# Attention scores in 128 by 128 tiles with wrapped keys, one masking addition over two PSUM banks and one maximum over all four blocks

## The chip, the cores and the metric

The kernel runs on one core of a Trainium2 chip. The core has five engines that the program drives separately: PE (TensorE, matrix products into PSUM), DVE (VectorE), ACT (ScalarE), POOL (GpSimd) and SP (SyncE, which only issues DMAs here). Each engine takes its instructions strictly in program order, and they meet through semaphores alone. The metric is the device time of one execution, in microseconds (us); lower is better. Three executions of the kernel before took 4307.14, 4308.0 and 4308.48 us, median 4308.0.

## The reference, cut to what matters

The input is 16 sequences of 256 tokens with 128 channels. After a layer norm it goes two ways: through one state-space block, and through six layers of windowed attention and feed-forward; the results are multiplied and added to the input. The change concerns the attention of the six layers, with 16 heads of 64 channels and windows of 32 tokens:

```python
bq = q.reshape(b, h, nw, w, d)                   # w = 32, nw = 8
bk2 = look(bk); bv2 = look(bv)                   # the window before, and the window itself: 64 keys
mask = (it < jb) | (it > jb + w) | (jb == -1)    # a query sees itself and the 32 tokens before it
sim = jnp.einsum('bhwie,bhwje->bhwij', bq, bk2) * QK_SCALE
sim = jnp.where(mask, -jnp.finfo(sim.dtype).max, sim)
attn = jax.nn.softmax(sim, -1)
out = jnp.einsum('bhwij,bhwje->bhwie', attn, bv2)
```

So each query sees 33 keys: a band along the diagonal. Everything is in float32.

## The kernel before, in words

The first 500 us or so are the layer norm and the state-space block. Then come six layers over eight groups of two sequences (512 tokens), 48 items in all. They are worked on in a software pipeline, function `turn`: one turn of 16 steps has up to four items in flight, `next` (projections of q and k, their squares and the rotation), `cur` (scores and probabilities), `prev` (output projection, layer norm, first half of the feed-forward) and `prev2` (end of the feed-forward). Every engine has its own `turn` with its own order within the 16 steps; nothing reorders them. In step s one pair of heads p = s // 2 of one sequence b = s % 2 has its scores computed.

One such unit, the two heads (index i) of one sequence (two halves t of 128 queries), goes through these places:

- `scores(s)`, PE: eight products of 64 queries by 96 keys (`SCORE_TILES`), head 0 into bank 0, head 1 into bank 1. They wait for `sc_bias`, which says that the maxima of step s - 1 have been read, since there is one pair of score banks. The first 128 columns are keys 0 to 127 of queries 0 to 127, the next 160 (to `UW` = 288) are keys 96 to 255 of queries 128 to 255.
- `maxima(s)`, DVE: four fused instructions (line 1240, in the profile CUSTOM_DVE_ANT_0) that add the mask, write the sum to `sm` and reduce it to its maximum, each followed by an instruction that reads the accumulator out to `mx` in bank 1; then a small product that makes the bias `nb` of the exponential.
- `probabilities(s)`, ACT: four exponentials from `sm` to `pr`, each with its sum into `den` (line 852).
- `denominators(s - 2)`, DVE: one reciprocal, `rden` (line 1219).
- `normalise(s - 2)`, POOL: four products with `rden` (line 964).
- `transpose_probs(s - 3)`, PE: four transposes of 128 by 128 into bank 2 (lines 634, 635). They wait for `p_Tsb`, which says that bank 2 has been copied out.
- `copy_probs(s - 4)`, DVE: a 32 by 32 transpose per head straight from `pr` (line 1225), for the keys 96 to 127 that queries 128 to 159 see, and one copy of bank 2 to `pt` (line 1226).
- `outputs`, PE, every second step: probabilities times `vtok`.

Around these, in each step s, DVE runs in this order: `denominators(s - 2)`, `copy_probs(s - 4)`, `products(s - 1)` (two products of 128x512 from PSUM with the rotation tables, line 1194, which wait for the projection of q or k), then in some steps `residual`, `scale_q` and others, then `maxima(s)`, then in some steps `clamp`, `gated`, `split_high_x` and `split_low_x`. PE runs `scores(s)`, `project_out` in steps 2 to 5, `transpose_probs(s - 3)`, `outputs` or the value projection `make_v`, the projection of q or k with three passes (lines 290 to 292), and feed-forward products in steps 12 to 15. A projection waits until ACT has squared what lay in its bank (`square`, line 840). In step 7 PE centres the layer norm's input (line 670), which a DMA brings after DVE's `residual` of step 6.

## Time and profile before

| | |
|---|---|
| median of 3 executions | 4308.0 us |
| the profiled execution, its own time | 4310.28 us |
| its span, first to last instruction | 4308.2 us |
| granted TensorE clock, mean | 0.956 of full speed |
| busy: PE, DVE, ACT, POOL | 85%, 84%, 71%, 63% |
| reciprocals `rden`, one for each step with scores | 768, so 48 turns of 16 steps |

The profile counts an engine as busy while an instruction of it runs. DVE's instructions overlap a little: one can start before the last has ended, so the time that one takes of the engine is the distance to the next start, and not its duration. A product in float32 is shown as two PE instructions (a row of x16 is eight products). "Idle before, releaser" is time in which the engine stood still, and the instruction on another engine that ended the wait; "issue" is a wait for which the profile shows no releaser.

### The profile page before, as it was taken

How to read it: one execution, taken by the hardware profiler on the slowest of the kernel's cores; microseconds unless marked ns; L12 is line 12 of the kernel's file. 1: busy time of each engine (PE TensorE's matmuls, PEld its weight loads, DVE VectorE, ACT ScalarE, POOL GpSimd, SP SyncE). 2: the span in 40 equal slices, each digit the busy share in tenths (PEclk: the TensorE clock that was granted, in tenths of full speed). 3: DMA queues.
4: the chain of work that ended last, by engine and by line, in shares of the span. 5: the costliest groups of instructions: out<-in, count | busy, mean ns of one | idle time of the engine just before them, and what ended most of it. 6: DMA issues, size and time to landing. Idle time of an engine off the chain costs nothing. (4 is left out here: it accounts for less than half of the span.)

```text
span 4308.2 us, 109724 instructions
## 1 busy us (share of the span) xinstructions
PE 3648.7 (85%) x31072; PEld 2319.1 (54%) x31072; DVE 3618.5 (84%) x12131; ACT 3063.5 (71%) x8807; POOL 2732.3 (63%) x4419
## 2 busy tenths in 40 slices
PE   5887688898888888888988888888888888898884
PEld 2444355555555555555555555555555555555552
DVE  7999688889888888888888888888887888888873
ACT  3443477777777777777787777777776777877774
POOL 0000577777777777677776776777776767777771
PEclk8999799999999999999999999999999999999997
DMA  1000322222222222222222222222222222222221
GB/s 45 6 7 12 106 92 90 85 90 96 90 88 90 82 95 93 87 93 84 84 101 91 93 87 80 88 95 88 99 84 79 94 95 89 94 85 89 86 78 61
DMA packets 225228, 352.55 MB, mean 82 GB/s; under 512 B 41535, under 2 KB 68349, under 8 KB 224381
## 3 DMA queue, kind: packets, MB, share of 16 engines
q1 hardware_dynamic: 224604, 345.22, 23.4%
q8 instruction: 271, 4.44, 0.4%
q14 instruction: 353, 2.88, 0.2%
HBM read 125.41 MB, written 5.77 MB: 30 GB/s over the span
## 5 line engine op out<-in xcount | busy, mean ns | idle before, releaser
L964 POOL TENSOR_SCALAR pr<-pr,rden 128x128 f32<-128x128 f32 (+1 forms) x3072 | 1134.4, 388 | 931.7 <-DVE rden L1219 930.6
L852 ACT ACTIVATE pr<-sm,nb,rq 128x128 f32<-128x128 f32 (+1 forms) x3072 | 1515.9, 498 | 44.7 <-DVE nb L1246 39.4
L971 POOL TENSOR_TENSOR rot<-ab,swp 128x512 f32<-128x512 f32 x768 | 984.4, 1282 | 509.7 <-DMA swp<-ab 508.5
L1194 DVE TENSOR_TENSOR ab<-bank,ltab 128x512 f32<-128x512 f32 x1536 | 985.4, 683 | 281.3 <-PE bank L292 260.8
L1240 DVE CUSTOM_DVE_ANT_0 sm<-bank,mask 128x128 f32<-128x128 f32 (+1 forms) x3072 | 841.3, 330 | 55.9 <-issue 52.2
L840 ACT ACTIVATE sq<-bank 128x512 f32<-128x512 f32 x768 | 451.6, 588 | 256.7 <-DVE ab L1194 255.0
L852 ACT ACTIVATION_READ_ACCUMULATOR pr<-sm,nb,rq 128x1 f32 x3072 | 587.8, 191 | 0.0
L634 PE MATMUL bank<-ident,pr 128*128 128x128 f32 x1536 | 407.1, 291 | 210.1 <-DVE pt L1226 208.3
L1226 DVE COPY pt<-bank 128x512 f32<-128x512 f32 x768 | 531.5, 692 | 10.2
L625 PEld LDWEIGHTS bank<-rot 64*64 64x64 f32 x12288 | 291.9, 133 | 452.8 <-issue 452.4
L977 POOL TENSOR_TENSOR rot<-rot,rkb 128x512 f32<-128x512 f32 x384 | 497.7, 1296 | 44.2 <-DMA rkb<-k_scratch 44.2
L861 ACT ACTIVATE wide<-bank 128x512 f32<-128x512 f32 x384 | 228.6, 595 | 383.4 <-PE bank L653 383.1
L625 PE MATMUL bank<-rot 64*64 64x96 f32 x12288 | 435.8, 257 | 76.7 <-DVE nb L1246 41.7
L653 PE MATMUL bank<-pt,vtok 128*64 128x160 f32 (+1 forms) x6144 | 491.2, 305 | 0.0
L290 PE MATMUL bank<-xh,wqk_h 128*128 128x512 f32 x768 | 358.9, 467 | 118.1 <-ACT sq L840 97.6
L1240 DVE DVE_READ_ACCUMULATOR2_ANT bank<- 128x1 f32 x3072 | 437.3, 142 | 0.0
L653 PEld LDWEIGHTS bank<-pt,vtok 128*64 128x64 f32 x6144 | 389.7, 143 | 72.3 <-issue 68.9
L634 PEld LDWEIGHTS bank<-ident,pr 128*128 128x128 f32 x1536 | 220.3, 143 | 361.8 <-issue 321.7
L866 ACT ACTIVATE vtok<-bank 128x512 f32<-128x512 f32 x384 | 228.3, 595 | 230.4 <-PE bank L292 230.3
L635 PE MATMUL bank<-ident,pr 128*128 128x128 f32 x1536 | 390.1, 280 | 0.0
L664 PE MATMUL bank<-wide,wo 128*128 128x512 f32 x768 | 371.0, 605 | 0.9 <-ACT wide L861 0.9
L292 PE MATMUL bank<-xl,wqk_h 128*128 128x512 f32 x768 | 309.2, 403 | 0.0
(156 smaller groups left out, 6503.7 us busy)
## 6 DMA issues: line engine op xcount, KB each, us to landing
swp<-ab SPq DMA_DIRECT2D x1536, 128.0 KB, 2.0
rkb<-k_scratch SPq DMA_DIRECT2D x768, 128.0 KB, 2.9
raw<-Wqkv SPq DMA_DIRECT2D x48, 128.0 KB, 2.2
gg<-xT SPq DMA_DIRECT2D x48, 128.0 KB, 2.3
gg<-xT SPq DMA_DIRECT2D x48, 127.5 KB, 2.4
raw<-Wqkv SPq DMA_DIRECT2D x12, 256.0 KB, 2.7
wo<-Wo SPq DMA_DIRECT2D x6, 512.0 KB, 4.2
k_scratch<-rsum SPq DMA_DIRECT2D x192, 8.0 KB
```

The costliest lines, as they stand in the source:

```text
L625: mm = pe.matmul(bank[i][part, c:c + 96], rot[rows, p, c0 + 64 * half:c0 + 64 * half + 64], rot[rows, PAIRS + p, c0 + k0:c0 + k0 + 96], st ...
L634: pe.transpose(bank[2][:, 256 * i:256 * i + P], pr[:, e % 4, i, 0:P], ident[:, :])
L635: mm = pe.transpose(bank[2][:, 256 * i + P:256 * i + 2 * P], pr[:, e % 4, i, P + WINDOW:UW], ident[:, :])
L653: mm = pe.matmul(bank[3][64 * i:64 * i + 64, cols], vtok[:, 2 * b + t, ch], pt[:, e % 4, i, t, 0:cols.stop - cols.start], start=(b == 0 an ...
L840: act.activation(sq[:, j % NSQ, :], use_bank("qk", j)[:, :], ACT.Square).then_inc(qk_sq, 1)
L852: ins = act.activation(pr[:, s % 4, i, cs], sm[:, s % 2, i, cs], ACT.Exp, bias=nb[:, s, t, i:i + 1], scale=head_scale(rq, p, b)[:, t, i:i ...
L964: ins = pool.tensor_scalar(pr[:, e % 4, i, cs], pr[:, e % 4, i, cs], rden[:, e, t, i:i + 1], 1.0, ALU.mult, ALU.mult)
L971: pool.tensor_tensor(rot[:, PAIRS * (j % 2) + j // 2, :], ab[:, j % 2, 0, :], swp[:, j % 2, :], ALU.add).then_inc(qk_rot, 1)
L977: pool.tensor_tensor(rot[:, PAIRS + p, :], rot[:, PAIRS + p, :], rkb[:, p % KSLOT, :], ALU.mult)\
L1194: ins = dve.tensor_tensor(seqs(ab[:, j % 2, i, :]), seqs(use_bank("qk", j)[:, :]), ltab[:, 2 * (j % 2) + i:2 * (j % 2) + i + 1, :] .to_bro ...
L1226: dve.tensor_copy(pt[:, e % 4, :, :, 0:P], bank[2][:, :].rearrange("p (i t c) -> p i t c", i=2, t=2)).then_inc(p_Tsb, 1)
L1240: ins = dve.tensor_tensor_reduce(sm[:, s % 2, i, cs], bank[i][:, cs], mask[:, cs], 1.0, -3e38, ALU.add, ALU.max, mx[:, t, i:i + 1])
```

## The change

`SCORE_TILES` gets a fourth field, the number of keys of a tile. Queries 128 to 191 now have two tiles: 64 keys from 128 on, and the 32 keys 96 to 127, which are put behind, into the last 32 columns of their block ("wrapped"; those queries cannot see keys 224 to 255, whose place it is). Each of the four blocks of scores is then 128 by 128, and the scores of a head lie in 256 columns. Banks 0 and 1 become one tensor `pair`, so that one instruction can cover both.

`maxima` is one addition of the mask over both banks to `sm`, then one `tensor_reduce` over the last axis for all four maxima into `mx` in PSUM, then the product that makes `nb`. The reduction waits for the addition on a new semaphore `sc_mask`.

`copy_probs` ends with a `memset` of 32 partitions by 2x32 elements: after the transposes of PE the wrapped probabilities also stand in `pt` where keys 224 to 255 of queries 128 to 159 belong, and they must be zero there. The `memset` waits for the copy on a new semaphore `p_copy`, and it is now what releases `p_Tsb`. `normalise` is one product over all 512 elements with `rden` broadcast. The exponentials are all 128 wide.

```diff
-SCORE_TILES = [(0, 0, 0), (1, 32, 32), (2, P, P - WINDOW), (3, P + 64, P + 32)]
+SCORE_TILES = [(0, 0, 0, 96), (1, 32, 32, 96), (2, P, P, 64), (2, 2 * P - WINDOW, P - WINDOW, WINDOW), (3, P + WINDOW, P + WINDOW, 96)]
...
-        mask = sb("mask", [P, UW])
+        mask = sb("mask", [P, 2 * P])
...
-        bank = [ctx.enter_context(nc.psum_tensor(f"bank{i}", [P, GT], F32)) for i in range(8)]
+        pair = ctx.enter_context(nc.psum_tensor("pair", [P, 2, GT], F32))
+        bank = [pair[:, 0, :], pair[:, 1, :]]
+        bank += [ctx.enter_context(nc.psum_tensor(f"bank{i}", [P, GT], F32)) for i in range(2, 8)]
...
-        mx = bank[1][:, UW:UW + 4].rearrange("p (t i) -> p t i", t=2)
+        mx = pair[:, 1, 2 * P:2 * P + 4].rearrange("p (i t) -> p i t", i=2)
...
-                    for half, c, k0 in SCORE_TILES:
+                    for half, c, k0, kn in SCORE_TILES:
                         part = slice(64 * (half % 2), 64 * (half % 2) + 64)
                         for i in range(2):
                             rows = slice(64 * i, 64 * i + 64)
-                            mm = pe.matmul(bank[i][part, c:c + 96], rot[rows, p, c0 + 64 * half:c0 + 64 * half + 64],
-                                           rot[rows, PAIRS + p, c0 + k0:c0 + k0 + 96], start=True, stop=True)
+                            mm = pe.matmul(bank[i][part, c:c + kn], rot[rows, p, c0 + 64 * half:c0 + 64 * half + 64],
+                                           rot[rows, PAIRS + p, c0 + k0:c0 + k0 + kn], start=True, stop=True)
...
                         pe.transpose(bank[2][:, 256 * i:256 * i + P], pr[:, e % 4, i, 0:P], ident[:, :])
                         mm = pe.transpose(bank[2][:, 256 * i + P:256 * i + 2 * P],
-                                          pr[:, e % 4, i, P + WINDOW:UW], ident[:, :])
+                                          pr[:, e % 4, i, P:2 * P], ident[:, :])
...
-                            cs = slice(0, P) if t == 0 else slice(P, UW)
+                            cs = slice(t * P, t * P + P)
                             ins = act.activation(pr[:, s % 4, i, cs], sm[:, s % 2, i, cs], ACT.Exp,
...
-                    for i in range(2):
-                        for t in range(2):
-                            cs = slice(0, P) if t == 0 else slice(P, UW)
-                            ins = pool.tensor_scalar(pr[:, e % 4, i, cs], pr[:, e % 4, i, cs],
-                                                     rden[:, e, t, i:i + 1], 1.0, ALU.mult, ALU.mult)
+                    dst = pr[:, e % 4, :, 0:2 * P].rearrange("p i (t c) -> p i t c", t=2)
+                    ins = pool.tensor_tensor(dst, dst, rden[:, e, :, :].rearrange("p t i -> p i t").unsqueeze(3)
+                                             .to_broadcast([P, 2, 2, P]), ALU.mult)
...
-                    dve.transpose(pt[96:128, e % 4, :, 0, P:P + WINDOW], pr[0:32, e % 4, :, P:P + WINDOW])
+                    dve.transpose(pt[96:128, e % 4, :, 0, P:P + WINDOW], pr[0:32, e % 4, :, 2 * P - WINDOW:2 * P])
                     dve.tensor_copy(pt[:, e % 4, :, :, 0:P],
-                                    bank[2][:, :].rearrange("p (i t c) -> p i t c", i=2, t=2)).then_inc(p_Tsb, 1)
+                                    bank[2][:, :].rearrange("p (i t c) -> p i t c", i=2, t=2)).then_inc(p_copy, 1)
+                    dve.wait_ge(p_copy, n16 + (16 * q + e + 1))
+                    dve.memset(pt[96:128, e % 4, :, 1, 0:WINDOW], 0.0).then_inc(p_Tsb, 1)
...
-                    for i in range(2):
-                        for t in range(2):
-                            cs = slice(0, P) if t == 0 else slice(P, UW)
-                            ins = dve.tensor_tensor_reduce(sm[:, s % 2, i, cs], bank[i][:, cs], mask[:, cs],
-                                                           1.0, -3e38, ALU.add, ALU.max, mx[:, t, i:i + 1])
-                    ins.then_inc(sc_max, 1)
+                    dst = sm[:, s % 2, :, 0:2 * P]
+                    dve.tensor_tensor(dst, pair[:, :, 0:2 * P], mask[:, :].unsqueeze(1).to_broadcast([P, 2, 2 * P]),
+                                      ALU.add).then_inc(sc_mask, 1)
+                    dve.wait_ge(sc_mask, n16 + (s + 1))
+                    dve.tensor_reduce(mx, dst.rearrange("p i (t c) -> p i t c", t=2), AX_X, ALU.max)\
+                        .then_inc(sc_max, 1)
                     dve.wait_ge(sc_max, n16 + (s + 1))
...
-                    dve.tensor_tensor(nb[:, s, :, :], mx, head_scale(nrq, p, b), ALU.mult).then_inc(sc_bias, 1)
+                    dve.tensor_tensor(nb[:, s, :, :], mx.rearrange("p i t -> p t i"), head_scale(nrq, p, b), ALU.mult).then_inc(sc_bias, 1)
```

The table `mask` is made to match. On DVE, one step (step 14 of a turn) reads like this before; ISA are the fused instructions and their accumulator reads:

```order
L1219 RECIPROCAL rden<-den 128x4 [waits p_exp]
L1224 REGISTER_ALU [waits p_T]
L1225 STREAM_TRANSPOSE pt<-pr 32x2x32 [waits o_ps]
L1226 COPY pt<-bank2 128x4x128
L1190 REGISTER_ALU
L1194 TENSOR_TENSOR ab<-bank5,ltab 128x512 [waits qk_rot,qk_proj]
L1194 TENSOR_TENSOR ab<-bank5,ltab 128x512
L1240 ISA sm,bank1<-bank0,mask 128x128 [waits p_exp,sc_ps,consts_made]
...
L1240 ISA sm,bank1<-bank1,mask 128x160
L1240 ISA bank1 128x1
L1246 TENSOR_TENSOR nb<-bank1,nrq 128x4 [waits sc_max]
```

The same step in the changed kernel. Its semaphores are given out in another order than their names, so the names shown are shifted: what is shown as sc_bias is `p_exp`, p_norm is `p_T`, and the p_T for which the MEMSET waits is `p_copy`; sc_mask and sc_max are what they say.

```order
L1219 RECIPROCAL rden<-den 128x4 [waits sc_bias]
L1224 REGISTER_ALU [waits p_norm]
L1225 STREAM_TRANSPOSE pt<-pr 32x2x32 [waits o_ps]
L1226 COPY pt<-bank2 128x4x128
L1229 MEMSET pt 32x2x32 [waits p_T]
L1190 REGISTER_ALU
L1194 TENSOR_TENSOR ab<-bank5,ltab 128x512 [waits qk_rot,qk_proj]
L1194 TENSOR_TENSOR ab<-bank5,ltab 128x512
L1240 TENSOR_TENSOR sm<-pair,mask 128x2x256 [waits sc_bias,sc_ps,consts_made]
L1243 TENSOR_REDUCE pair<-sm 128x4 [waits sc_mask]
L1248 TENSOR_TENSOR nb<-pair,nrq 128x4 [waits sc_max]
```

Eight instructions between the products and `nb` have become two, the second of which waits for the first, and one with a wait has come between the copy and the products. On PE, the scores of one step and what follows them read like this before:

```order
L625 MATMUL bank0<-rot 64x96 [waits sc_bias,consts_made]
L625 MATMUL bank1<-rot 64x96
L625 MATMUL bank0<-rot 64x96
L625 MATMUL bank1<-rot 64x96
L625 MATMUL bank0<-rot 64x96
L625 MATMUL bank1<-rot 64x96
L625 MATMUL bank0<-rot 64x96
L625 MATMUL bank1<-rot 64x96
L634 MATMUL bank2<-ident,pr 128x128 [waits p_Tsb,p_norm]
L635 MATMUL bank2<-ident,pr 128x128
```

And like this now (p_copy is `sc_bias` here):

```order
L627 MATMUL pair<-rot 64x96 [waits p_copy,consts_made]
L627 MATMUL pair<-rot 64x96 x3
L627 MATMUL pair<-rot 64x64 x2
L627 MATMUL pair<-rot 64x32 x2
L627 MATMUL pair<-rot 64x96 x2
```

Ten products stand where eight stood, with the same number of columns in all; nothing else has moved on PE.

## Rows read from the trace of the kernel before

**Rows 1.** The page, part 1: busy us of the engines, share of the span.

```profile
PE 3648.7 (85%) x31072; PEld 2319.1 (54%) x31072; DVE 3618.5 (84%) x12131; ACT 3063.5 (71%) x8807; POOL 2732.3 (63%) x4419
```

**Rows 2.** Waits, 1000 to 4000 us: engine, tile, line, releaser: us, times, longest.

```profile
DVE ab L1194 <- PE bank L292: 194.2, 200, 3.0
PE bank L634 <- DVE pt L1226: 168.0, 126, 3.5
```

**Rows 3.** Timeline of DVE, steps 10 and 11 of a turn: start, us, line, operation, count.

```profile
2009.86 1.28 DVE L1194 TENSOR_TENSOR ab<-bank,ltab 128x512 f32<-128x512 f32 x2
2011.06 0.28 DVE L1240 CUSTOM_DVE_ANT_0 sm<-bank,mask 128x128 f32<-128x128 f32 x1
...
2012.26 0.16 DVE L1246 TENSOR_TENSOR nb<-bank,nrq 128x4 f32<-128x4 f32 x1
2012.34 0.17 DVE L1219 RECIPROCAL rden<-den 128x4 f32<-128x4 f32 x1
...
2012.79 0.69 DVE L1226 COPY pt<-bank 128x512 f32<-128x512 f32 x1
2013.39 1.28 DVE L1194 TENSOR_TENSOR ab<-bank,ltab 128x512 f32<-128x512 f32 x2
```

**Rows 4.** The page, part 5: the fused instruction and its accumulator read.

```profile
L1240 DVE CUSTOM_DVE_ANT_0 sm<-bank,mask 128x128 f32<-128x128 f32 (+1 forms) x3072 | 841.3, 330 | 55.9 <-issue 52.2
...
L1240 DVE DVE_READ_ACCUMULATOR2_ANT bank<- 128x1 f32 x3072 | 437.3, 142 | 0.0
```

**Rows 5.** Timeline of DVE at the start of the program.

```profile
10.67 4.42 DVE L1039 TENSOR_REDUCE rsum<-rot 128x32 f32<-128x4096 f32 x1 [9.34 <-DMA rot<-x_in]
15.13 0.18 DVE L1040 TENSOR_SCALAR rsum<-rsum 128x32 f32<-128x32 f32 x1
```

**Rows 6.** DVE's instructions by line, 0 to 60 us: busy us, mean ns, idle before.

```profile
L1047 DVE TENSOR_TENSOR rot<-rot,rsum 128x4096 f32<-128x4096 f32 x1 | 4.4, 4426 | 1.8 <-ACT rsum L759 1.8
L1044 DVE TENSOR_REDUCE rsum<-rot 128x32 f32<-128x4096 f32 x1 | 4.4, 4422 | 3.7 <-ACT rot L755 3.7
L1031 DVE MEMSET mean_w<- 128x128 f32 x1 | 0.2, 165 | 0.8 <-PEq L1406 0.8
```

**Rows 7.** One line at a time, whole run: durations in ns, minimum, median, maximum.

```profile
L1194 DVE TENSOR_TENSOR ab<-bank,ltab x1536: 661/681/694, 445.0 to 4163.0; 128x512 f32<-128x512 f32 x192
L1176 DVE TENSOR_TENSOR xl<-xT,xh x48: 673/2446/3145, 425.9 to 4073.3; 64x512 fp32r<-64x512 f32 x48
```

**Rows 8.** Timeline of PE at the scores of one step.

```profile
2001.06 0.56 PE L625 MATMUL bank<-rot 64*64 64x96 f32 x16
2001.55 0.33 PE L634 MATMUL bank<-ident,pr 128*128 128x128 f32 x1
```

**Rows 9.** The page, part 5: two groups of POOL: busy us, mean ns, idle before.

```profile
L964 POOL TENSOR_SCALAR pr<-pr,rden 128x128 f32<-128x128 f32 (+1 forms) x3072 | 1134.4, 388 | 931.7 <-DVE rden L1219 930.6
L971 POOL TENSOR_TENSOR rot<-ab,swp 128x512 f32<-128x512 f32 x768 | 984.4, 1282 | 509.7 <-DMA swp<-ab 508.5
```

**Rows 10.** Timeline of DVE over one turn: rows with a wait, in brackets.

```profile
2088.01 0.29 DVE L1240 CUSTOM_DVE_ANT_0 sm<-bank,mask 128x128 f32<-128x128 f32 x1 [0.83 <-issue]
...
2104.50 1.29 DVE L1194 TENSOR_TENSOR ab<-bank,ltab 128x512 f32<-128x512 f32 x2 [0.87 <-PE bank L292]
2116.27 1.29 DVE L1194 TENSOR_TENSOR ab<-bank,ltab 128x512 f32<-128x512 f32 x2 [1.48 <-PE bank L292]
...
2149.30 1.29 DVE L1194 TENSOR_TENSOR ab<-bank,ltab 128x512 f32<-128x512 f32 x2 [0.37 <-PE bank L292]
```

**Rows 11.** Timeline of PE over the same turn: rows with a wait.

```profile
2099.55 0.30 PE L634 MATMUL bank<-ident,pr 128*128 128x128 f32 x1 [1.62 <-DVE pt L1226]
...
2119.65 0.47 PE L290 MATMUL bank<-xn_h,w_h 128*85 128x512 f32 x1 [0.44 <-DVE gg L1259]
2127.67 0.50 PE L290 MATMUL bank<-xh,wqk_h 128*128 128x512 f32 x1 [0.38 <-ACT sq L840]
2155.16 1.13 PE L670 MATMUL bank<-gg,center_w 128*128 128x512 f32 x2 [1.31 <-DMA gg<-xT]
```

More of the change, by code:

```diff
@@ L211, in build @@
         k_norm = sem("k_norm")
-        sc_ps, sc_max, sc_bias, p_exp, p_rden, p_norm, p_T, p_Tsb, o_ps, o_sb = (
-            sem(n) for n in ("sc_ps", "sc_max", "sc_bias", "p_exp", "p_rden", "p_norm", "p_T", "p_Tsb", "o_ps", "o_sb"))
+        sc_ps, sc_mask, sc_max, sc_bias, p_exp, p_rden, p_norm, p_T, p_copy, p_Tsb, o_ps, o_sb = (
+            sem(n) for n in ("sc_ps", "sc_mask", "sc_max", "p_copy", "sc_bias", "p_exp", "p_rden", "p_norm", "p_T", "p_Tsb", "o_ps", "o_sb"))
         at_out, at_add = sem("at_out"), sem("at_add")
@@ L224, in build @@
         credited = [x_hi, x_split, qk_proj, qk_sq, qk_mul, qk_rot, sq_part, sq_clamp,
[L225 removed]
+                    r_ln, r_exp, v_proj, v_sb, rq_T, rq_sb, k_norm, sc_ps, sc_mask, sc_max, p_copy, sc_bias,
                     p_exp, p_rden, p_norm, p_T, p_Tsb, o_ps, o_sb, at_out, at_add, f_cen, f_xc, f_sq, f_var,
@@ L1358, in constants @@
     own = np.arange(P)[None, :]
-    wide = np.arange(P + WINDOW)[None, :] - WINDOW
+    wrapped = np.where((q < 64) & (own >= P - WINDOW), own - P, own)
     def band(k):
         return np.where((k > q) | (k < q - WINDOW), MASKED, 0.0)
-    mask = np.concatenate([band(own), band(wide)], 1)
+    mask = np.concatenate([band(own), band(wrapped)], 1)
     headsum = np.zeros((P, 2, 32))
```

1 line of the change is left out of this document (removed).

## Prediction

> **What bounds the kernel now.** I read the shares of busy time first. PE is busy 85% of the span and DVE 84%, ACT 71% and POOL 63% [rows 1]: two engines are nearly full, and an average can't say which of them decides. So I read who waits for whom. In the 3000 us from 1000 to 4000 us DVE's rotation products wait 194.2 us for PE's projections, and PE's transposes wait 168.0 us for DVE's copy of bank 2 [rows 2]. Both waits are there because the lead changes within a turn. The timelines of one turn show where. Here the reader is to look at what has no bracket. DVE last waited at 2088.01 us, at the maxima of step 9; then it has next to nothing to wait for up to the products of step 13 (2104.50, 0.87 us), and then up to those of step 15 (2116.27, 1.48 us) [rows 10]. In this part PE is the one that waits: 1.62 us for the copy at 2099.55, 0.44 us for `gated` at 2119.65, and 0.38 us for a square, which in turn waited for DVE's products, at 2127.67 [rows 11]. From 2127.67 to the centring matmul at 2155.16, 27.5 us, no row of PE has a wait: there PE leads, with the output projection and the values, and DVE waits in nearly every second step. So steps 9 to 15 and 0, about half a turn, belong to DVE, and steps 1 to 8 to PE. A change on DVE counts in full in the first part, and in the second only where it is larger than DVE's wait.
>
> There are 1536 rotation products [rows 7], two in a step, so 768 steps with scores, 48 turns of 16.
>
> **Maxima.** Before, the first fused instruction starts at 2011.06 and the product `nb` at 2012.26 [rows 3]: 1.20 us of the engine, though the durations of four pairs, 4 x (330 + 142) ns [rows 4], add up to 1.89 us; each starts before the last has ended. The addition that replaces them has a PSUM and an SBUF input and 512 elements, like the rotation product: median 0.681 us [rows 7]. The reduction has no row at this size, but over 4096 elements it takes 4422 ns, and a two-input product of that length 4426 [rows 6]: equal. So I take 0.69 us for 512. Each is waited for by the next; a reduction that started at 10.67 and took 4.42 us was followed by its reader at 15.13 [rows 5], a gap of 0.04 us. Together 0.69 + 0.04 + 0.69 + 0.04 = 1.46 us, 0.26 more than now. Nothing hides a reduction that waits for the addition, and `nb` waits behind it, with ACT's exponentials and PE's next scores behind `nb`.
>
> Bounds: with no gaps and the shortest row, 0.661 us [rows 7], twice, 1.32 us, still 0.12 more; with 0.694 twice and both gaps, 0.27 more. No row allows a gain as long as the reduction takes one element at a time. Far above stands contention: DVE's difference `xl`, with two SBUF inputs and 64x512, took 0.673 us at best and 2.446 in the median [rows 7]. The products with one input in PSUM never passed 0.694 [rows 7] with POOL busy 63% of the time [rows 1], and the reduction's rows are from a time when POOL was idle. I take no contention.
>
> The Trainium skill, SBUF — State Buffer, section "Who interferes with whom", says that on this chip `tensor_reduce` never contends with GpSimd for the shared port, while an operation with two SBUF inputs does. By that rule the reduction stays at 0.69 us; the rows on `xl` and on the PSUM products agree with its second half, and no row here can show the first.
>
> **Memset.** The copy starts at 2012.79 and the products at 2013.39, 0.60 us later, before its 0.69 are over [rows 3]. Now the memset waits for the copy: 0.69 + 0.04, then 64 elements. A memset of 128 elements took 0.165 us [rows 6]; I take 0.11, and 0.03 until the products start, since the memset must end first. That is 0.87 us, 0.27 more. Bounds: 0.15 with a memset near nothing, 0.33 with 0.165. PE's transposes wait for `p_Tsb`, and so for the memset too.
>
> Sum on DVE: 0.53 us a step. All of it in the open would be 768 x 0.53 = 407 us.
>
> **Scores on PE.** The first score product starts at 2001.06 and the first transpose at 2001.55 [rows 8]: 0.49 us for eight. Columns are the same, but there are ten products; if instructions set the pace, 0.49 x 2/8 = 0.12 us more, if columns do, nothing. I take 0.1. It counts where PE leads.
>
> **POOL and ACT.** Four products at 388 ns make 1.55 us; one two-input product of 512 takes 1.28 [rows 9]: 0.27 us shorter. POOL stands idle 930.6 us before this line, waiting for `rden` [rows 9], so nothing that a shorter product would release is late; even 1 us more would find that cover. The exponentials read 32 columns less in two of four, a few hundredths of a us. I count both at nothing.
>
> **Along one turn.** I add the pieces in order, 0.26 for each maxima and 0.27 for each memset on the path.
> - Steps 9 to 13. Maxima of 9, 10 and 11 (0.78), memsets of 10, 11 and 12 (0.81): 1.59 at the copy for which PE waits. From there the path runs over PE to the products of step 13; DVE's own second branch grows by 0.53 and its wait there was 0.87, so it stays behind.
> - Steps 13 to 15. Maxima of 13: 0.26, in all 1.85. DVE then adds 0.27 + 0.26 + 0.27 = 0.80 up to the products of step 15, under its wait of 1.48 there. The path goes by ACT, which has the gelu. Nothing more.
> - Steps 15 to 1. Maxima of 15 release `gated`, on which PE waits: 0.26. Memset of 0, maxima of 0, memset of 1 come before the products that the square at 2127.67 needs: 0.80. In all 2.91.
> - PE's part. Six score phases up to 2155.16: 0.6. At 2149.30 DVE's wait is 0.37 [rows 10], and a maxima and a memset, 0.53, have come since its last: the residual of step 6 is 0.16 late. PE waits 1.31 us for the DMA behind it [rows 11], so this counts. Two more score phases: 0.2. DVE's other waits here are as long as what is added.
>
> In all 3.87 us of a turn; DVE's whole addition is 16 x 0.53 = 8.5, so 5.7 of it disappears in its waits (the 0.8 of PE is not part of it). 48 x 3.87 = 186 us. The profiled execution took 4310.3 us; with 186 it is 4496, and the median of the runs lies 2.3 us lower. In some turns an issue wait at the turn's edge swallows a few tenths. I forecast 4492 us.
>
> The forecast's own bounds: with 0.12 for the maxima, 0.15 for the memset and nothing on PE, 6 x 0.12 + 5 x 0.15 = 1.47 us a turn, 71 us, 4379. With 0.27, 0.33 and 0.12: 1.62 + 1.65 + 0.96 + 0.23 for the residual = 4.46 us, 214 us, 4522.
>
> **Rivals.**
> - *The added work stands in the open almost everywhere.* For it: the waits change places from turn to turn, and DVE's idle time in PE's part (about 0.6 a step) is hardly more than 0.53. Against: PE shows 27.5 us without a wait, which DVE's delay must first fill. At the worst 16 x 0.53 + 16 x 0.1 = 10.1 us a turn, 485 us, 4793; half of what I called hidden gives 3.87 + 2.8 = 6.7, 320 us, 4630. A reduction slowed by POOL would look the same: at 0.5 us more, six times a turn on the path, 144 us more, 4636. Together 0.12.
> - *The waits swallow it.* DVE's 16% of idle time is 0.16 x 4.9 = 0.8 us a step, more than 0.53. For it: the plain average. Against: the idle time isn't in steps 9 to 12, where the maxima are chained. Time 4308 to 4330. Chance 0.06.
> - *Fewer instructions win.* If what a DVE instruction costs were its duration, the maxima would fall from 1.89 us to 0.69 + 0.69 = 1.38, and with the memset the path would change by 6 x (-0.51) + 5 x 0.27 = -1.71 us a turn: 82 us faster, 4226. It decides from the point where the fused chain occupies more than 1.46 us. Against: 1.20 us from its first start to `nb` [rows 3]. Chance 0.05.
> - *The change doesn't do what it says* on POOL: the broadcast product is slower than an even one, and PE's transposes wait for it. POOL has 63% x 4.9 = 3.1 us of work in a step; only from about 1.8 us more does it become full, and by then it would add that excess to every step: at 0.2 us, 154 us on top of nothing else, 4650. Chance 0.03.
>
> The Trainium skill, VectorE: DVE Perf Modes, section "Rules for kernel authors", advises to minimise the number of DVE operations, because each is followed by a flush, and the same section says to expect one element per cycle of `tensor_reduce` and to restructure. The first half would speak for the third rival; the starts of the fused instructions in this trace speak against it, since they lie closer than their durations. The second half agrees with the row of the reduction, 4422 ns for 4096 elements.
>
> **How the numbers follow.** Forecast 0.74, rivals 0.12, 0.06, 0.05, 0.03. A difference of 0.2% (9 us) is what a measurement here can tell from none. Slower: forecast, first and fourth, and half of the second: 0.92. Same: the other half, 0.03. Faster 0.05. The range takes in the forecast's bounds and reaches to the first rival's half case: 4370 to 4600.
>
> **What would show it.** The step from the first instruction of the maxima to `nb` should be 1.40 to 1.50 us in place of 1.20, and from the copy to the products 0.80 to 0.90 in place of 0.60. DVE's share should rise to about 90%, PE's busy share fall. PE's wait for `pt` should grow, and DVE's wait for PE's projections shrink to half or less. The scores should take 0.5 to 0.6 us up to the first transpose. It would be wrong if the maxima took 1.2 us or less, if the reduction's duration spread with POOL's work, or if PE still had 27 us without a wait and a turn were nevertheless 5 us longer.

## The result, and the profile after

The changed kernel takes 4510.01 us, median of 4 executions (4506.23 to 4516.61); the kernel before took 4308.24 in the same comparison. The ratio is 1.0467, with a 95% interval from 1.045 to 1.0484: 4.7% or 202 us slower. The forecast was 4492. The total is close, but how it is made up is not what the prediction said, as the experiments show: misses that cancel had their part in it.

The page of the changed kernel, its head and part 1, beside [rows 1]; the columns are those of the page before:

```profile
span 4504.4 us, 109726 instructions
PE 3768.5 (84%) x34144; PEld 2456.6 (55%) x34144; DVE 3846.5 (85%) x8291; ACT 3055.5 (68%) x8807; POOL 2390.4 (53%) x2117
```

The span grew by 196.2 us, 4.09 us for each of the 48 turns. DVE issues 3840 instructions fewer and is busy 228 us more. Its share hardly rises, from 84 to 85%, since the span grew with it.

The timeline of DVE in two steps in which it waits for nothing, beside [rows 3]:

```profile
2005.03 0.68 DVE L1240 TENSOR_TENSOR sm<-pair,mask 128x512 f32<-128x512 f32 x1
2005.75 0.69 DVE L1243 TENSOR_REDUCE pair<-sm 128x4 f32<-128x512 f32 x1
2006.47 0.16 DVE L1248 TENSOR_TENSOR nb<-pair,nrq 128x4 f32<-128x4 f32 x1
...
2007.00 0.69 DVE L1226 COPY pt<-bank 128x512 f32<-128x512 f32 x1
2007.77 0.11 DVE L1229 MEMSET pt<- 32x64 f32 x1
2007.91 1.29 DVE L1194 TENSOR_TENSOR ab<-bank,ltab 128x512 f32<-128x512 f32 x2
```

From the first instruction of the maxima to `nb` it is 1.44 us (1.20 before, 1.46 predicted). From the copy to the products it is 0.91 (0.60 before, 0.87 predicted): the memset takes 0.11 as estimated, but the gaps before and behind it are 0.08 and 0.03, in place of 0.04 and 0.03.

Four lines of the changed kernel over the whole run, durations in ns, minimum, median, maximum, beside [rows 7]; the last two groups are also part of what follows:

```profile
L1243 DVE TENSOR_REDUCE pair<-sm x768: 694/695/697, 496.8 to 4414.0; 128x4 f32<-128x512 f32 x192
L964 POOL TENSOR_TENSOR pr<-pr,rden x768: 1035/1041/1055, 501.7 to 4420.3; 128x512 f32<-128x512 f32 x192
L1176 DVE TENSOR_TENSOR xl<-xT,xh x48: 682/684/1544, 426.7 to 4264.4; 64x512 fp32r<-64x512 f32 x48
L1169 DVE CAST xh<-xT x48: 408/1330/1526, 425.8 to 4253.5; 64x512 fp32r<-64x512 f32 x24, 64x512 fp32r x24
```

The reduction takes 0.695 us and never spreads, though POOL works beside it half of the time. The Trainium skill (SBUF — State Buffer, "Who interferes with whom") has it that `tensor_reduce` does not contend with GpSimd on this chip; these 768 instructions agree. POOL's single product takes 1.04 us where 1.28 was expected. And two lines that the change does not touch have moved: the difference `xl` fell from a median of 2446 ns [rows 7] to 684, and the first cast of `xh` rose from 613 to 1330.

The waits of PE from 1000 to 4000 us (us, times, longest), beside [rows 2]:

```profile
PE bank L636 <- POOL pr L964: 152.6, 102, 3.2
PE bank L292 <- ACT sq L842: 101.3, 90, 2.5
PE pair L627 <- DVE nb L1248: 58.1, 74, 1.9
```

The row that said that PE's transposes wait for DVE's copy now names POOL's product. Read as it stands, it says that POOL has become the bound of the transposes and that the memset does not matter. Both had to be tested.

The clock has moved too. The trace has the clock granted to TensorE, which stands at one of two levels, 2.4 GHz or 1.2 GHz. The mean over the run fell from 0.956 to 0.937 of full speed. Averaged over 44 turns, each taken from PE's first score product in step 0 to the next, PE spent 5.20 us of a turn at 1.2 GHz before and 8.69 us after. Of that, 2.02 and 4.39 us lie in step 12, between PE's scores of step 12 and those of step 13.

### The profile page after: what moved, and what is told of

The parts are those of the page before. It is cut to its first block and busy times, and to the rows that moved or that the text cites. A ratio compares the mean times of both kernels' runs of the same rounds, so it can differ in the third digit from the quotient of the medians.

```text
span 4504.4 us, 109726 instructions
## 1 busy us (share of the span) xinstructions
PE 3768.5 (84%) x34144; PEld 2456.6 (55%) x34144; DVE 3846.5 (85%) x8291; ACT 3055.5 (68%) x8807; POOL 2390.4 (53%) x2117
## 5 line engine op out<-in xcount | busy, mean ns | idle before, releaser
L964 POOL TENSOR_TENSOR pr<-pr,rden 128x512 f32<-128x512 f32 x768 | 799.8, 1041 | 1414.3 <-DVE rden L1219 1355.0
L854 ACT ACTIVATE pr<-sm,nb,rq 128x128 f32<-128x128 f32 x3072 | 1474.9, 484 | 84.5 <-DVE nb L1248 82.6
L971 POOL TENSOR_TENSOR rot<-ab,swp 128x512 f32<-128x512 f32 x768 | 982.2, 1279 | 505.4 <-DMA swp<-ab 496.5
L627 PEld LDWEIGHTS pair<-rot 64*64 64x64 f32 x15360 | 378.8, 135 | 496.7 <-issue 496.3
L636 PE MATMUL bank<-ident,pr 128*128 128x128 f32 x1536 | 421.5, 299 | 207.9 <-POOL pr L964 202.6
L627 PE MATMUL pair<-rot 64*64 64x96 f32 (+2 forms) x15360 | 478.9, 248 | 113.8 <-DVE nb L1248 74.5
L1243 DVE TENSOR_REDUCE pair<-sm 128x4 f32<-128x512 f32 x768 | 533.9, 695 | 26.6
L1240 DVE TENSOR_TENSOR sm<-pair,mask 128x512 f32<-128x512 f32 x768 | 523.4, 682 | 18.2 <-issue 15.4
L655 PE MATMUL bank<-pt,vtok 128*64 128x160 f32 (+1 forms) x6144 | 509.3, 313 | 0.0
L655 PEld LDWEIGHTS bank<-pt,vtok 128*64 128x64 f32 x6144 | 403.3, 147 | 76.6 <-issue 71.0
L637 PE MATMUL bank<-ident,pr 128*128 128x128 f32 x1536 | 401.8, 286 | 0.0
L293 PE MATMUL bank<-xh,wqk_l 128*128 128x512 f32 x768 | 314.4, 409 | 0.0
```

The lines of the kernel that those rows point to most:

```text
L627: mm = pe.matmul(bank[i][part, c:c + kn], rot[rows, p, c0 + 64 * half:c0 + 64 * half + 64], rot[rows, PAIRS + p, c0 + k0:c0 + k0 + kn], st ...
L636: pe.transpose(bank[2][:, 256 * i:256 * i + P], pr[:, e % 4, i, 0:P], ident[:, :])
L655: mm = pe.matmul(bank[3][64 * i:64 * i + 64, cols], vtok[:, 2 * b + t, ch], pt[:, e % 4, i, t, 0:cols.stop - cols.start], start=(b == 0 an ...
L854: ins = act.activation(pr[:, s % 4, i, cs], sm[:, s % 2, i, cs], ACT.Exp, bias=nb[:, s, t, i:i + 1], scale=head_scale(rq, p, b)[:, t, i:i ...
L964: ins = pool.tensor_tensor(dst, dst, rden[:, e, :, :].rearrange("p t i -> p i t").unsqueeze(3) .to_broadcast([P, 2, 2, P]), ALU.mult)
L971: pool.tensor_tensor(rot[:, PAIRS * (j % 2) + j // 2, :], ab[:, j % 2, 0, :], swp[:, j % 2, :], ALU.add).then_inc(qk_rot, 1)
```

## The experiments

All ratios are to the kernel before, run on the same chip in the same comparison; "us" is the ratio's difference from 1, or between two ratios, times 4308. The kernel before had medians from 4308.2 to 4314.8 us in these comparisons. The casts are the sum of the two lines that cast `xh` in DVE's step 11 (or 8), whole run, from the profiles. The last two columns are from the profiles too: us of a turn in which TensorE's granted clock was 1.2 GHz, and how much of that lay in step 12, average of 44 turns.

| kernel | median us | ratio, 95% interval | casts us | at 1.2 GHz | in step 12 |
|---|---|---|---|---|---|
| before | 4308.2 | 1 | 68.1 | 5.20 | 2.02 |
| the change | 4510.0 | 1.0467, 1.045 to 1.0484 | 87.4 | 8.69 | 4.39 |
| e1_memset | 4419.9 | 1.0241, 1.022 to 1.0262 | 105.9 | 7.68 | 3.79 |
| e2_fused | 4409.1 | 1.0216, 1.0189 to 1.0242 | 105.8 | 7.37 | 3.72 |
| e3_nomemset | 4411.5 | 1.0219, 1.0195 to 1.0242 | 102.4 | 6.83 | 3.39 |
| e4_pool4 | 4532.3 | 1.0498, 1.0474 to 1.0523 | 107.9 | 9.77 | 4.34 |
| e5_scores | 4313.3 | 0.9996, 0.9985 to 1.0007 | 68.5 | 5.12 | 1.71 |
| e6_pool2 | 4356.6 | 1.0108, 1.0091 to 1.0124 | 103.4 | 6.36 | 4.09 |
| e7_before_cast8 | 4268.2 | 0.9891, 0.987 to 0.9912 | 49.5 | 3.41 | 0.00 |
| e8_after_cast8 | 4409.7 | 1.0219, 1.0202 to 1.0236 | 43.2 | 6.44 | 0.02 |
| e9_cast8_pool2 | 4209.5 | 0.9768, 0.9749 to 0.9787 | 49.3 | 2.64 | 0.00 |
| e10_cast8_memset | 4304.9 | 0.9986, 0.9974 to 0.9998 | 48.5 | 4.03 | 0.00 |
| e11_after_copyfrees | 4488.2 | 1.0415, 1.0395 to 1.0436 | 86.2 | 8.53 | 3.72 |
| e12_after_cast8_fused | 4262.2 | 0.9883, 0.9861 to 0.9905 | 46.9 | 3.34 | 0.01 |

### One part at a time

**e1_memset**: the kernel before with the memset, which here clears columns of `pt` that nothing reads.

```diff
...
-                                    bank[2][:, :].rearrange("p (i t c) -> p i t c", i=2, t=2)).then_inc(p_Tsb, 1)
+                                    bank[2][:, :].rearrange("p (i t c) -> p i t c", i=2, t=2)).then_inc(p_copy, 1)
+                    dve.wait_ge(p_copy, n16 + (16 * q + e + 1))
+                    dve.memset(pt[96:128, e % 4, :, 1, P:P + WINDOW], 0.0).then_inc(p_Tsb, 1)
```

> The kernel before with one thing added: the memset of 32 partitions by 2x32 elements, which waits for the copy of bank 2 and now releases PE's transposes (here into columns of pt that nothing reads). Theory: 0.27 us more from the copy to the products, on the path at 5 places of a turn, 5 x 0.27 x 48 = 65 us, so about 4373 us (4360 to 4395). Rival 'hidden': what releases PE's transposes is POOL's normalisation, as the waits of the changed kernel say, so the memset is nearly free: under 4325. Rival 'all in the open': 768 x 0.27 = 207 us, 4515.

Measured +104 us. The memset is far from free, so the "hidden" rival is out, but 104 is more than the 65 that the count gives.

**e2_fused**: the changed kernel with `tensor_tensor_reduce` on four blocks of 128 columns.

```diff
-                    dve.tensor_tensor(dst, pair[:, :, 0:2 * P], mask[:, :].unsqueeze(1).to_broadcast([P, 2, 2 * P]),
-                                      ALU.add).then_inc(sc_mask, 1)
-                    dve.wait_ge(sc_mask, n16 + (s + 1))
-                    dve.tensor_reduce(mx, dst.rearrange("p i (t c) -> p i t c", t=2), AX_X, ALU.max)\
-                        .then_inc(sc_max, 1)
+                    for i in range(2):
+                        for t in range(2):
+                            cs = slice(t * P, t * P + P)
+                            ins = dve.tensor_tensor_reduce(sm[:, s % 2, i, cs], bank[i][:, cs], mask[:, cs],
+                                                           1.0, -3e38, ALU.add, ALU.max, mx[:, i, t:t + 1])
+                    ins.then_inc(sc_max, 1)
```

> The changed kernel with the four fused instructions back in the maxima, on four blocks of 128 columns; tiles, memset and POOL's single product as in the changed kernel. From the first fused instruction to nb it should take about 1.14 us where the changed kernel takes 1.44. Theory: that is on the path at 6 places of a turn, 6 x 0.30 x 48 = 86 us, so about 4424 us (4400 to 4450). Rival 'all in the open': 768 x 0.30 = 230 us, 4280. Rival 'the memset or POOL made it': above 4480.

Measured 108 us less than the change (1.0467 - 1.0216), against 86 expected, although the casts take 18 us more here.

**e3_nomemset**: the changed kernel without the memset. It leaves the wrapped probabilities standing in `pt`.

```diff
-                                    bank[2][:, :].rearrange("p (i t c) -> p i t c", i=2, t=2)).then_inc(p_copy, 1)
-                    dve.wait_ge(p_copy, n16 + (16 * q + e + 1))
-                    dve.memset(pt[96:128, e % 4, :, 1, 0:WINDOW], 0.0).then_inc(p_Tsb, 1)
+                                    bank[2][:, :].rearrange("p (i t c) -> p i t c", i=2, t=2)).then_inc(p_Tsb, 1)
```

> The changed kernel without the memset and its wait (the zeroing of the wrapped probabilities is left out). Theory: 5 x 0.27 x 48 = 65 us less, about 4445 us (4425 to 4470). Rival 'POOL releases the transposes' (in the trace of the changed kernel PE waits 202.6 us for POOL's line 964 and 2.3 us for the memset): no change, 4500 to 4515. If the memset is the true releaser, PE's transposes should start 0.15 us after the end of the copy instead of 0.15 us after the end of the memset.

Measured 107 us less than the change. PE's first wait from 1000 to 4000 us in this kernel:

```profile
PE bank L636 <- DVE pt L1226: 149.9, 86, 3.3
```

POOL has the same product here as in the changed kernel, and its name is gone from the row. The timeline of the changed kernel shows how it got in, at the transposes of step 12, POOL and DVE first, then PE:

```profile
2022.33 1.04 POOL L964 TENSOR_TENSOR pr<-pr,rden 128x512 f32<-128x512 f32 x1 [1.07 <-DVE rden L1219]
2023.23 0.11 DVE L1229 MEMSET pt<- 32x64 f32 x1
2023.49 0.30 PE L636 MATMUL bank<-ident,pr 128*128 128x128 f32 x1 [2.71 <-POOL pr L964]
```

POOL ends at 2023.37, the memset at 2023.34. Both answer one reciprocal, and copy plus memset happen to be as long as POOL's product, which belongs to the next unit. PE starts 0.15 us after the memset's end. The rival by which POOL releases the transposes expected no change here; it is out.

**e4_pool4**: the changed kernel with four POOL products.

```diff
-                    dst = pr[:, e % 4, :, 0:2 * P].rearrange("p i (t c) -> p i t c", t=2)
-                    ins = pool.tensor_tensor(dst, dst, rden[:, e, :, :].rearrange("p t i -> p i t").unsqueeze(3)
-                                             .to_broadcast([P, 2, 2, P]), ALU.mult)
+                    for i in range(2):
+                        for t in range(2):
+                            cs = slice(t * P, t * P + P)
+                            ins = pool.tensor_scalar(pr[:, e % 4, i, cs], pr[:, e % 4, i, cs],
+                                                     rden[:, e, t, i:i + 1], 1.0, ALU.mult, ALU.mult)
```

> The changed kernel with four POOL products of 128 elements per unit instead of the single one of 512 (about 1.5 us of POOL instead of 1.04). Theory: POOL is off the path, 4500 to 4520 us. Rival 'POOL releases the transposes': 0.45 us later at steps 10 and 12 of each turn, 2 x 0.45 x 48 = 43 us slower, about 4553. A second thing to look at is the cast of xh in step 11 (L1169, 0.61 us in the median before, 1.33 in the changed kernel) and the difference xl in step 13 (2.45 before, 0.68 in the changed kernel): if they depend on what POOL is doing at that moment, they should move here again, up to 0.7 us of a turn, 34 us.

Measured 13 us more than the change, with intervals that overlap (from 1.0474 here, up to 1.0484 there): between the expectations. But the casts are 20 us longer: they moved, as the second thing to look at had it, though `xl` did not. That made the casts a suspect.

**e5_scores**: the kernel before with ten score products; the loop of `scores` takes the number of keys from the fourth field, as in the change.

```diff
-SCORE_TILES = [(0, 0, 0), (1, 32, 32), (2, P, P - WINDOW), (3, P + 64, P + 32)]
+SCORE_TILES = [(0, 0, 0, 96), (1, 32, 32, 96), (2, P + WINDOW, P, 64), (2, P, P - WINDOW, WINDOW), (3, P + 64, P + 32, 96)]
...
```

> The kernel before with ten score products a step instead of eight (the 96 keys of queries 128 to 191 in two pieces of 32 and 64), nothing else. In the changed kernel the distance from the first score product to the first transpose is 0.55 us where it was 0.49. Theory: 0.06 us at the 8 steps in which PE leads, 8 x 0.06 x 48 = 23 us, 4331 (4315 to 4345). Rival 'columns set the pace': no change, 4308. Rival 'the predicted 0.1 us': 38 us, 4346.

Measured no difference, -2 us (interval -6 to +3). The two rows of PE that answer to [rows 8], from this kernel:

```profile
2005.25 0.61 PE L625 MATMUL bank<-rot 64*64 64x96 f32 x20
2005.79 0.33 PE L634 MATMUL bank<-ident,pr 128*128 128x128 f32 x1
```

0.54 us in place of 0.49: the price of a step is there, and it adds up to nothing that can be seen. Averaged over 44 turns, PE's steps 2 to 6 are 0.20 us longer, and step 7, where PE waits for the DMA before the centring, is 0.25 us shorter: that wait takes back what the scores add. The theory's 23 us are out, and so is the reading that all of PE's stretch counts.

**e6_pool2**: the kernel before with two broadcast POOL products.

```diff
-                    for i in range(2):
-                        for t in range(2):
-                            cs = slice(0, P) if t == 0 else slice(P, UW)
-                            ins = pool.tensor_scalar(pr[:, e % 4, i, cs], pr[:, e % 4, i, cs],
-                                                     rden[:, e, t, i:i + 1], 1.0, ALU.mult, ALU.mult)
+                    for t in range(2):
+                        cs = slice(0, P) if t == 0 else slice(P, UW)
+                        dst = pr[:, e % 4, :, cs]
+                        ins = pool.tensor_tensor(dst, dst, rden[:, e, t, :].unsqueeze(2)
+                                                 .to_broadcast([P, 2, P if t == 0 else P + WINDOW]), ALU.mult)
```

> The kernel before with two broadcast POOL products a unit (2x128 and 2x160 elements) instead of four. POOL should need about 1.25 us a unit instead of 1.46. Theory: POOL is off the path, and only where DVE's casts and differences with SBUF operands meet POOL can the time move: between -20 and +20 us, 4288 to 4328. What decides is the sum of the casts of xh (L1169 and L1170, 68 us in the kernel before): the time should move with it. Rival 'POOL releases the transposes': faster by 0.2 us x 48 x 3, 30 us, with the casts unchanged.

Measured 46 us slower, more than expected on that side, although POOL's line fell from 1134 to 993 us. The casts went from 68 to 103 us, as expected of them, and with them the time at 1.2 GHz in step 12 doubled.

### The casts

In `split_high_x`, DVE casts 64x512 twice, from SBUF to SBUF, in step 11. In e1_memset, the two casts and what POOL does then:

```profile
2066.29 0.42 DVE L1169 CAST xh<-xT 64x512 fp32r x1
2066.72 1.39 DVE L1170 CAST xh<-xT 64x510 fp32r x1
```

```profile
2064.93 1.46 POOL L964 TENSOR_SCALAR pr<-pr,rden 128x128 f32<-128x128 f32 x4
2066.36 1.47 POOL L971 TENSOR_TENSOR rot<-ab,swp 128x512 f32<-128x512 f32 x1
2067.79 1.45 POOL L996 TENSOR_TENSOR xn_l<-gg,xn_h 128x512 fp32r<-128x512 f32 x1
```

The first cast began 0.07 us before POOL's sum and took 0.42. The second, of the same size, met it and took 1.39, to 0.3 us after that sum's end. In the changed kernel the first cast met one:

```profile
2020.08 1.46 DVE L1169 CAST xh<-xT 64x512 fp32r x1
2021.56 0.42 DVE L1170 CAST xh<-xT 64x510 fp32r x1
```

```profile
2019.99 1.27 POOL L996 TENSOR_TENSOR xn_l<-gg,xn_h 128x512 fp32r<-128x512 f32 x1
```

A page of the Trainium skill states this rule (SBUF — State Buffer, "Who interferes with whom": a DVE cast in a mode that uses two ports and a GpSimd instruction exclude each other for the whole of an instruction). The rows agree: the second cast ended 0.3 us after the sum, and the sum that overlapped the first cast took 1.47 us, where its mean in this kernel is 1.28. In the kernel before, much of the collision fell on `xl` in step 13, 109.7 us in the run [rows 7 has its median], and DVE had time there: its products of step 15 still waited 1.48 us [rows 10]. In e1, e2, e3, e4 and e6, which delay DVE or change POOL's work, `xl` takes 40 to 43 us and the casts 34 to 40 us more than before: the collision has moved to step 11, where DVE leads.

**e7_before_cast8** and **e8_after_cast8**: the kernel before and the changed kernel, with

```diff
-                    if gs[2] is not None and s == 11:
+                    if gs[2] is not None and s == 8:
```

> The kernel before with the two casts of xh moved from step 11, where DVE leads, to step 8, where DVE waits for PE (1.16 us at the transposes and 0.57 us at the products, on the average of 25 turns). Theory: the casts (68 us in all, 1.4 us a turn) leave the leading stretch, of which step 9's wait on PE gives part back: 40 to 68 us faster, 4240 to 4270. Rival 'the turn is bound by the sum of DVE's work': no change, 4300 to 4315, since the work stays.

> The changed kernel with the same move of the casts to step 8. Theory: the part of the loss that is not the maxima or the memset is the casts' meeting with POOL in step 11; DVE's slack at step 8 is 0.80 us here and takes part of the casts only. The casts of 1.8 us a turn leave step 11, and 0.3 to 1 us of them reappears at steps 8 and 9: 40 to 70 us faster than the changed kernel, 4440 to 4470. Rival 'the casts do not matter': 4505 to 4515.

Measured -47 us for e7, as expected, though DVE's work is the same. For e8, -107 us against the change: more than the 87 us that the casts took there. The trace shows what else was gained. PE in step 12, from the transposes on, in the changed kernel and then in e8:

```profile
2023.49 0.30 PE L636 MATMUL bank<-ident,pr 128*128 128x128 f32 x1 [2.71 <-POOL pr L964]
...
2024.05 2.12 PE L655 MATMUL bank<-pt,vtok 128*64 128x160 f32 x16
2026.10 0.80 PE L292 MATMUL bank<-xn_h,w_h 128*128 128x512 f32 x1
```

```profile
2075.04 0.30 PE L636 MATMUL bank<-ident,pr 128*128 128x128 f32 x1 [0.63 <-DVE pt L1229]
...
2075.60 1.20 PE L655 MATMUL bank<-pt,vtok 128*64 128x160 f32 x16
2076.73 0.50 PE L292 MATMUL bank<-xn_h,w_h 128*128 128x512 f32 x1
```

The same two stretches as windows, up to the scores of step 13: length, busy time of PE, of its weight loads (PEld), of DVE, ACT and POOL, then the granted clock as a share of 2.4 GHz, DMA share and GB/s:

```profile
2023.49:2028.37 4.88, 4.88 (x27) 3.57 (x27) 3.95 (x11) 2.76 (x9) 4.11 (x4) 0.65 0.27 91
```

```profile
2075.04:2078.32 3.28, 3.28 (x26) 2.40 (x26) 3.17 (x10) 2.21 (x7) 3.28 (x4) 1.00 0.20 77
```

In the changed kernel the casts in front of the copy kept PE waiting for 2.71 us. The granted clock of the 4.88 us that follow is 0.65 of full speed, so most of them stood at 1.2 GHz, and the same products took 1.6 us longer. In e8 the wait was 0.63 us and the clock stayed at 2.4 GHz. All five kernels with the casts in step 8 spend next to nothing of step 12 at 1.2 GHz, the others 1.7 to 4.4 us. Per turn, e8 is 1.99 us shorter than the change: PE stands still 1.09 us less and runs 0.90 us less. No run holds the clock and moves the casts, so how much of e8's gain is the clock's is a reading of the trace.

For five pairs of kernels, the same account in us of a turn, averages of 44 turns. The lower level is half the upper, so at most half of the last column is time lost by the clock:

| pair | turn | PE idle | PE running | time at 1.2 GHz |
|---|---|---|---|---|
| before to change | +4.05 | +1.68 | +2.37 | +3.49 |
| before to e1 (memset) | +2.34 | +1.22 | +1.12 | +2.48 |
| before to e6 (POOL) | +0.83 | +0.42 | +0.41 | +1.16 |
| before to e7 (casts) | -0.91 | -0.28 | -0.63 | -1.78 |
| e8 to e12 (maxima) | -3.24 | -1.83 | -1.41 | -3.10 |

**e9_cast8_pool2**: e7 with e6's edit of POOL.

> The kernel before with the casts of xh in step 8 and POOL's two broadcast products instead of four. The two broadcast products alone made it 1.1% slower, with 35 us more in the casts. Theory: they did so only by moving POOL's work onto the casts in step 11; with the casts in step 8 they cost nothing, 4268 us (4255 to 4285), the same as the casts' move alone. Rival 'the faster POOL product itself costs': again 40 us or more, above 4305.

Measured -53 us against e7 (0.9768 - 0.9891): the same edit that cost 46 us with the casts in step 11 gains 53 with them in step 8. The theory was right in the sign of what the collision did, and wrong that nothing else hangs on POOL. With the casts in step 8, DVE's products wait for POOL's rotation and PE's feed-forward for `xn_l`; two rows of e7's waits, DVE and PE, 1000 to 4000 us:

```profile
DVE ab L1194 <- POOL rot L971: 35.6, 38, 1.4
```

```profile
PE bank L290 <- POOL xn_l L996: 15.2, 29, 0.8
```

In e9 the first is 20.8 us and the second does not appear, and `xl` takes 120 us where it took 143. Together these two waits shrink by 30 us in the 3000 us of the window; that they make the gain is not shown. This is the fastest kernel of the study, 2.3% faster than the one before.

**e10_cast8_memset**: e7 with e1's edit.

> The kernel before with the casts in step 8 and the memset of the changed kernel. The memset alone cost 2.4%, 104 us, where the prediction's count gives 65. Theory: the other 38 us were the casts, which met POOL; with the casts in step 8 the memset costs 5 x 0.27 x 48 = 65 us over 4268: 4333 (4318 to 4350). Rival 'the memset is on the path at 8 places, not 5': 104 us, 4372.

Measured +41 us against e7 (0.9986 - 0.9891). With the casts in step 8 the memset costs 41, not 104, and less than the 65 of the count. The 63 us between are more than the 38 that the casts grew by in e1: there the time at 1.2 GHz also grew by 2.48 us of a turn, here by 0.62.

**e11_after_copyfrees**: the changed kernel, and

```diff
-                    pe.wait_ge(p_Tsb, n16 + (16 * q + e))
+                    pe.wait_ge(p_copy, n16 + (16 * q + e))
```

> The changed kernel, where PE's transposes wait for the copy of bank 2 and no longer for the memset behind it (the products with v still wait for the memset). The memset stays in DVE's queue. Theory: the memset costs as time of DVE, 0.27 us each; PE's wait for it is 0.15 us at one or two places of a turn: 7 to 15 us faster than the changed kernel, 4495 to 4503. Rival 'what costs is that PE waits for the memset': most of the 100 us come back, below 4430. Rival of the wait row 'POOL releases the transposes': nothing changes.

Measured -22 us against the change, a little more than expected, and the row of the transposes changes its name again, with POOL untouched:

```profile
PE bank L636 <- DVE pt L1226: 136.6, 98, 2.8
```

Leaving the memset out gave 107 us (e3), and freeing PE from waiting for it gives 22: it costs by its place in DVE's queue more than by PE's wait.

**e12_after_cast8_fused**: e8 with e2's edit.

> The changed kernel with the casts in step 8 and the four fused instructions in the maxima; memset, ten score products and POOL's single product stay. Theory: 0.30 us at 6 places of a turn, 86 us less than the changed kernel with the casts moved (4410): 4324 (4300 to 4345). Against the casts' move alone (4268) that leaves the memset's 65 us and next to nothing for scores, POOL and ACT. Rival 'the maxima in the open everywhere': 4180.

Measured 4262, 145 us less than e8 (1.0219 - 0.9883). From the first fused instruction to `nb` it takes 1.13 us here:

```profile
2004.27 0.28 DVE L1242 CUSTOM_DVE_ANT_0 sm<-pair,mask 128x128 f32<-128x128 f32 x1
...
2005.40 0.16 DVE L1248 TENSOR_TENSOR nb<-pair,nrq 128x4 f32<-128x4 f32 x1
```

So 0.31 us a step make 145 / 48 = 3.0 us of a turn. If all of it were places at which the 0.31 us counts, there would be about ten, not six. But the table of pairs has another part: PE stands still 1.83 us less of a turn, as much as six places give (1.86), and runs 1.41 us less, with 3.10 us less at 1.2 GHz. The runs do not separate more places from a lower clock. The waits of DVE in e12 and in e8, 1000 to 4000 us:

```profile
DVE ab L1194 <- PE bank L294: 160.7, 178, 3.4
DVE pt L1225 <- PE bank L637: 77.6, 135, 3.3
```

```profile
DVE ab L1194 <- PE bank L294: 137.5, 121, 3.0
DVE pt L1225 <- PE bank L637: 17.9, 24, 1.9
```

Of DVE's waits for the transposes, most of which lie in PE's part, e8 has hardly any left, so some of the longer maxima may have come to count there. In steps 9 to 14 DVE hardly waits in either kernel, but the products of step 15 wait about 2.0 us in e12 and 2.3 in e8, and that wait can still hide a delay of steps 13 and 14.

## Why the prediction was right, and where its parts were not

- **What bounds the kernel: right.** DVE leads in steps 9 to 15 and 0, PE in 1 to 8. Moving the casts between the two parts, with all work kept, gives 47 us (e7), though part of that is the clock in step 12. The rival in which all added work stands in the open (0.53 us in 768 steps, 407 us) fell with the total of 202; so did the one in which the waits swallow it.
- **Price of the maxima: right.** 1.44 us against 1.46, 0.24 more than before. The rival by which fewer instructions win is out with the same rows: the four pairs start closer than their durations, and two dependent instructions do not. e2 and e12 show it at 108 and 145 us the other way.
- **Price of the memset: a little low**, 0.31 in place of 0.27.
- **Where the count along the turn failed: luck in the total.** The prediction has 3.87 us of a turn, and measured are 4.05, average of 44 turns. Split at PE's scores: steps 9 to 12 grew by 3.09 us, where the count has 1.59 up to the copy of step 12; steps 13 and 14 shrank by 0.26, where it adds 0.26; steps 15, 0 and 1 grew by 1.07, where it has 1.06; and steps 2 to 8, PE's part, grew by 0.15, where it has 0.96. The part that DVE leads costs more than was said and PE's part nearly nothing, and the two misses cancel. In steps 9 to 12 the casts are 0.4 us of a turn longer (19 us in 48 turns); much of the rest can be the clock, as the next point says.
- **What the count left out: the granted clock.** No term of it stands for a slower TensorE. PE runs 2.37 us of a turn longer in the changed kernel. In e5 the ten score products alone make 0.61 of that, which its waits take back. The time at 1.2 GHz grew by 3.49 us, 2.76 of it in steps 9 to 12; half of that is 1.74 us of a turn, an estimate from this trace of the running time that it adds. It comes behind PE's longer waits in step 12 (2.53 us of idle time before, 3.35 after).
- **"Maxima at six places, 0.26 each", 75 us.** e2 and e12 changed the maxima by 0.31 us. Scaled to the 0.24 between before and after, their 108 and 145 us are 84 and 112, more than the count. The count took DVE's waits and PE's clock as fixed. Whether each place that uses up a wait makes the next one count, or the clock makes the rest, is open. The memset shows the same: 41 us on a kernel whose DVE still waits and whose clock stays high in step 12 (e10), 107 on the changed one (e3).
- **"I take no contention" was right for the new instructions and wrong for the old ones.** The reduction and the addition don't contend. The casts of step 11, which the change doesn't touch, took 19 us more in the change, and 34 to 40 in e1, e2, e3, e4 and e6. The prediction had the row of `xl`, and read it only as a bound for the reduction.
- **"POOL at nothing": the wrong reason for a small number.** Two products in place of four cost 46 us (e6) or gain 53 (e9), by where the casts stand. In the change the single product against four is worth 13 us, which its intervals hardly tell from none.
- **Scores at 0.1 us in eight steps, 38 us: too high.** 0.05 to 0.06 us a step, and nothing in the total (e5): PE's wait for the DMA in step 7, which the prediction let cover nothing, covers them.
- **The sum.** Taken out of the changed kernel one at a time, the maxima are worth 108 us and the memset 107, 215 together where the whole is 202 (the fused instructions put back are 0.07 us a step shorter than those before). Put into the kernel before one at a time, the memset costs 104, POOL's two products 46 and the scores -2; with the 108 that is 256. The casts are in it: they grow by 38 us with the memset alone and by 35 with POOL's edit alone, but by 19 in the change. With the casts in step 8 the same sum of parts, -47 + 41 - 53 - 2 = -61 us, has to meet e12, which is at -50. That is near, but e12 has POOL's single product and the shorter fused instructions on 128 columns, and neither was measured alone there. The 145 us up to e8 are a difference of runs, and test nothing.
- **Two slips in the working.** Of DVE's 8.5 us, 3.07 are counted on the path, so that 5.4 disappear and not 5.7. And the fourth rival's 4650 us is the forecast with 154 us on top, not "on top of nothing else", which gives 4462.
- **Of the signs named ahead**, the two distances on DVE, the score products' 0.55 us, PE's lower busy share (84%, before 85) and the lower waits for PE's projections came true (165.5 us after, 194.2 before [rows 2]); these did not shrink to half. DVE's share did not reach 90%. PE's wait for `pt` did not grow: 168.0 us before, 152.6 after, under POOL's name. What grew are PE's waits for squares, from 61.4 to 101.3 us, and for `nb`, from 34.2 to 58.1. And PE still has its stretch without a wait, 28.5 us long (2052.97 to 2081.47), in a turn that is 4.05 us longer: short of the 5 us at which the prediction would have called itself wrong.

What stays open: how many places of a turn the maxima cost, as against the clock, what the clock alone is worth, and what makes e9's gain beyond the two wait rows.

## What to carry to other kernels

Replacing fused instructions by fewer, larger ones on the engine that leads gains only if the larger ones are shorter from start to start: two instructions of which the second waits for the first pay both in full, and a wait chained behind a copy costs its gaps too. A count of the places where such a price is paid is a count with all else fixed: look at what a longer wait does to the engine that waits. Here PE's granted clock fell behind its longest wait, and its next products took 1.6 us longer. Waits that take back a delay further on, such as PE's in step 7, have to be counted as well. And look for what the delay moves together: an instruction that nobody touched, but that excludes another engine, can be worth as much as the edit itself, and moving it to a step where its engine has time gained 47 us on the kernel before and 107 on the changed one, as much as taking out the memset or the new maxima did.

## What the runs showed of the hardware that was not expected

- After 2.71 us in which PE waited, its granted clock was 0.65 of full speed over the next 4.88 us: eight products (x16) took 2.12 us instead of 1.20, one pass of 128x512 0.80 instead of 0.50. After 0.63 us of waiting at the same place it stayed at 2.4 GHz (e8).
- A cast of 64x512 from SBUF to SBUF took 0.42 us alone and 1.39 to 1.46 us when it met an instruction of POOL.
- POOL's product with a broadcast operand, 128x512, took 1.041 us; its products of two full operands of that size took 1.28 (L971). Four products of 128 columns with a per-partition scalar took about 1.41 us (e4).
- A memset of 32x64 that waits for the copy before it started 0.07 to 0.08 us after that copy's end; the reduction started 0.04 after the addition that it waits for.
- A wait row can name an instruction that ended at nearly the same time, and not the one that the semaphore waited for. The same wait was put down to POOL in the changed kernel and to DVE in e3, e4 and e11.
